# A causal attention layer's prologue reordered: value copies on ScalarE, second-batch products in other banks and among the first maxima, stacks loaded by parts, centring done one stage earlier

## The chip, the cores and the metric

The kernel runs on one core of one Trainium2 chip. The metric is the device time of one execution in microseconds (us); lower is better. TensorE multiplies, VectorE and ScalarE work elementwise and reduce, GpSimd fills constants and does some elementwise work, SyncE (SP) issues the DMAs.

## The reference, cut to what matters

The program is a decoder of two layers over x of shape (2, 1024, 256). Layer 0 has linear attention, a cross attention and a recurrence; layer 1 has causal attention with 16 heads of 16 dimensions, attention to a short context, and a routed mixture of experts. What the change touches is the end of the recurrence and the start of the causal attention:

```python
h = layernorm(x)                              # over the 256 features
q, k, v = h @ Wq + bq, h @ Wk + bk, h @ Wv + bv   # 16 heads of 16
scores = q @ k.T / sqrt(16)                   # per batch and head, 1024 x 1024
probs = softmax(where(causal, scores, -inf))
x = x + (probs @ v) @ Wout + bout
```

The line is a summary; the kernel computes it with features on the partitions and tokens along the free dimension (`c.xT`, 128 x 2 x 2048).

## The kernel before, in words

Each layer is a stage with a block of its own, in which each engine has one written-out order of instructions, tied to the others by semaphores; a stage starts on all engines when the one before has ended. The tokens fall into four chunks of 512 (`ch` 0 to 3; 0 and 1 are batch 0).

**The end of the recurrence** (`cross_attention_and_recurrence`). TensorE's order ends with `mean(bn, 0)`, `mean(bn, 1)`, `variance(bn, 0)`, `outputs(1, 1)` and `variance(bn, 1)` (L1163 to L1168): the statistics of the next norm, for batch 0 alone. VectorE adds the outputs to x (`add_output`, L1434), sums both feature halves (`add_halves`, L1398), centres chunks 0 and 1 (`centre`, L1402) and multiplies them by the inverse root (`normalise_tokens`, L1409). ScalarE makes the roots (L1225, L1228).

**The prologue of the causal layer** (`causal_attention_layer`). TensorE makes the means of the late chunks 2 and 3 (L1793), the queries of batch 0 (L1813, banks 0 to 3), the variances of the late chunks (L1804), the keys (L1813, banks 4 to 7) and the values (L1820, banks 0 to 3 again, once the queries are read); then the same for batch 1: queries into banks 0 to 3, each once VectorE has copied the values of batch 0 out of the bank (`v_copied`), keys into banks 4 to 7, and values into banks 0 to 3. An f32 product of 128 x 512 is two passes on TensorE, so four products of two halves are 16 passes. VectorE centres the late chunks (L2020), ScalarE squares them (L1958) and, between queries and keys, takes their roots (`late_roots`, L1963 and L1966), and VectorE scales them (L2026).

ScalarE reads queries and keys out of PSUM with their bias (L1977). For batch 0 it then makes the splitting copies: each of q and k is cut into three bf16 parts, the first two by ScalarE (L1986), each followed by VectorE's subtraction (L2032, then L2034, which writes the third). GpSimd does the same for batch 1 later (L1775 to L1781), once batch 0's parts are stored. VectorE copies the values of both batches into `v_aug` (L2041), after its last subtraction.

SP stores the six parts of batch 0 to DRAM (L1724), waits for all six, and loads them back as stacks (`loads`, L1717 and L1719): a quad is four heads, its stack of q and of k holds six blocks of 16 partitions, block r being part `Q_PART[r]` or `K_PART[r]`:

```python
Q_PART = (0, 0, 0, 1, 1, 2)
K_PART = (0, 1, 2, 0, 1, 0)
```

So a quad is twelve DMAs of 128 KB. Quad 0 and quad 1 are issued one after the other, then SP waits for the first shift rows (`keep_shift`, L1730), then issues quad 2, whose stack lies where the normalised tokens were, so that it waits for the last values. There are three stacks for the eight quads of both batches.

**The main loop.** Before TensorE can make a score (L1860), the row maxima of that half must be known. A maximum product or "piece" (`piece`, L1838 with a mask product L1841) is reduced by VectorE (L2051); after the eleven pieces of the first half VectorE splits the negated maxima (`split_shift`, L2065, L2067), TensorE turns them (L1848), VectorE copies them out (L2074) and SP's two small DMAs put them as two rows under the query stack (L1730). Rows of ones under the key stacks are GpSimd's memsets (L1766 for the first two stacks, L1770 for the third, which lies in the weights' room and waits for the last values). `count_pieces` plans how many pieces stand before each score; twelve stand before the first. TensorE's order ahead of the loop, before:

```python
pe.wait_ge(*s["masks"](2))
pe.wait_ge(*s["k_ones"](2))
pe.wait_ge(*pr["k_raw"](4))
pe.wait_ge(*pr["v_copied"](4))
more_pieces(0, upto[0])
```

`k_ones` reaches 2 with GpSimd's second memset. The pieces go through a ring of four banks (4 to 7), the scores through banks 0 to 2. ScalarE takes the exponentials (L1994) and TensorE multiplies them with the values (L1875).

Of the kernel before, what the change touches and what calls it, by code (L numbers as in the profile page):

```python
# [28 lines left out]
P = 128  # L29
# [668 lines left out]
def cross_attention_and_recurrence(nc, c):  # L698
# [42 lines left out]
    with ExitStack() as ctx:  # L741
# [81 lines left out]
        with nc.Block() as block:  # L823
# [46 lines left out]
            def _(pe):  # L870
# [297 lines left out]
                variance(bn, 1)  # L1168

# [140 lines left out]
            def _(dve):  # L1310
# [251 lines left out]
                add_output(1, 1)  # L1562
                for ch in (0, 1):
                    normalise_tokens(bn, ch)
# [3 lines left out]
def causal_attention_layer(nc, c):  # L1568
# [81 lines left out]
    with ExitStack() as ctx:  # L1650
        bn, yn = c.bn, c.yn
        pr = c.signals(nc, "bp", dict(q_proj=4, k_proj=4, v_proj=4, q_raw=4, k_raw=4, v_copied=4))
        s = c.signals(nc, "b", dict(part=0, rest=0, last_part=0, stored=0, later_part=0, later_stored=0, ones=0, masks=0, k_ones=0,
                                       loaded0=0, loaded1=0, loaded2=0, shifted0=0, shifted1=0, made=0, read=0,
                                       max_step=0, parts=0, scored=0, expd=0, av=0, out_copied=0, inv=0))
        set_round(0, s)
        loaded = [s["loaded0"], s["loaded1"], s["loaded2"]]
        shifted = [s["shifted0"], s["shifted1"]]
        sb = lambda name, shape, dt=F32: ctx.enter_context(nc.sbuf_tensor(name, shape, dt))
# [42 lines left out]
        with nc.Block() as block:  # L1702

            @block.sync
            def _(sync):
                def loads(n):
                    b, quad = divmod(n, QUADS)
                    a = n % 3
                    if n == 2:
                        pr["v_proj"].round = 1  # L1710
                        sync.wait_ge(*pr["v_proj"](4))
                    if n >= 3:
                        sync.wait_ge(*s["scored"](QUAD * first_group(2 * (n - 2))))
                    by_head = lambda ap: ap.rearrange("(h d) n -> d h n", d=DH)
                    rows = slice(quad * QUAD * DH, (quad + 1) * QUAD * DH)
                    for r in range(len(Q_PART)):
                        sync.dma_start(qs[a][r * DH:(r + 1) * DH], by_head(q_dram[b, Q_PART[r], rows, :]))\  # L1717
                            .then_inc(loaded[a].sem, 16)
                        sync.dma_start(ks[a][r * DH:(r + 1) * DH], by_head(k_dram[b, K_PART[r], rows, :]))\  # L1719
                            .then_inc(loaded[a].sem, 16)  # L1720
# [34 lines left out]
            def _(pool):  # L1755
# [11 lines left out]
                pr["v_proj"].round = pr["q_raw"].round = pr["k_raw"].round = 1  # L1767
                pool.wait_ge(*pr["v_proj"](4))
                pool.wait_ge(*s["k_ones"](1))
                pool.memset(ks[2][ROWS:ROWS + SHIFT], 1.0).then_inc(s["k_ones"].sem)  # L1770
                pool.wait_ge(*s["stored"](6 * 16))
                pool.wait_ge(*s["k_ones"](2))
                for n, (raw, parts, ready) in enumerate(((raw_of[1][0], q_parts, pr["q_raw"]), (raw_of[1][1], k_parts, pr["k_raw"]))):
                    pool.wait_ge(*ready(4))
# [7 lines left out]
                pool.wait_ge(*s["later_part"](8))  # L1782
                for ch in range(3):
# [6 lines left out]
            def _(pe):  # L1790
                for ch in LATE:
                    pe.wait_ge(*bn["sum"](ch + 1))
                    pe.matmul(norm_bank(ch), c.mean_w[:], factor(ch), start=True, stop=True).then_inc(bn["mean"].sem)  # L1793
                for b in range(B):
                    set_round(b, pr)
                    xn = lambda k, first, n: xn_all[:, k, b * S + first:b * S + first + n]
                    for name, base, done in (("b_wq", 0, pr["q_proj"]), ("b_wk", 4, pr["k_proj"])):
                        for n in range(4):
                            m, j = divmod(n, NCH)
                            if b == 0 and base and n == 0:  # L1800
                                for ch in LATE:
                                    pe.wait_ge(*bn["sq"](ch + 1))
                                    for k in range(FT):
                                        mm = pe.matmul(norm_bank(ch), c.mean_w[:], squares[ch][:, k, :], start=(k == 0), stop=(k == 1))  # L1804
# [1694 lines left out]
```

## Time and profile before

| what | value |
|---|---|
| three runs | 1653.85, 1656.48, 1660.8 us |
| median | 1656.48 us |
| the profiled execution's own time | 1651.91 us |
| its span | 1650.2 us |
| mean granted TensorE clock in it | 0.968 |
| busy in the span | TensorE 93%, VectorE 58%, ScalarE 44%, GpSimd 23% |

The profile is of one execution, in us from the start of its span. "PE" is TensorE's multiplying, "PEld" its loading of weights, DVE is VectorE, ACT ScalarE, POOL GpSimd, SP or SPq SyncE and its queue of DMAs. A granted clock of 1.00 is the full 2.4 GHz, 0.50 is 1.2 GHz. L1838 is line 1838 of the kernel. The causal layer starts at 708.3 us.

### The profile page before, as it was taken

What the parts mean: (1) busy time and instruction counts of PE and PEld (TensorE: products, weight loads), DVE (VectorE), ACT (ScalarE), POOL (GpSimd) and SP (SyncE); (2) the same over time, 40 slices, a digit from 0 to 9 for tenths busy, and PEclk for the clock granted to TensorE, in tenths of its full rate; (3) what the DMA queues carried; (4) which work ended last, traced back from release to release, by engine and by line L of the source; (5) the groups of instructions that cost most, each with busy time, mean ns of one, the idle gap of its engine ahead of it and who ended that gap; (6) DMA issues with size and microseconds to landing.
All of it is one profiled execution on the core that took longest, in us unless ns stands there. A gap on an engine that the chain in (4) does not pass through costs nothing. (4 is left out here: it accounts for less than half of the span.)

```text
span 1650.2 us, 19104 instructions
## 1 busy us (share of the span) xinstructions
PE 1533.0 (93%) x6998; PEld 838.9 (51%) x7002; DVE 962.3 (58%) x1491; ACT 718.6 (44%) x1256; POOL 372.2 (23%) x300
## 2 busy tenths in 40 slices
PE   6989999998999999977999999889879999999998
PEld 3744444432222234434454544332358888888886
DVE  4642124767675652343978776368579575564753
ACT  4345232453334333251466566533555444545441
POOL 0000000122221210034200000110216655655561
PEclk9989999999999999987999999989999999999998
DMA  6000000000000000017255330000302332312201
GB/s 274 1 1 0 0 0 4 1 0 1 1 0 1 1 0 0 0 68 98 28 128 67 40 40 2 1 4 1 103 26 77 98 100 73 103 65 88 84 9 51
DMA packets 38707, 67.54 MB, mean 41 GB/s; under 512 B 3864, under 2 KB 19288, under 8 KB 38232
## 3 DMA queue, kind: packets, MB, share of 16 engines
q1 hardware_dynamic: 38616, 66.33, 15.6%
q8 instruction: 56, 0.92, 0.2%
q14 instruction: 35, 0.29, 0.1%
HBM read 57.80 MB, written 8.39 MB: 40 GB/s over the span
## 5 line engine op out<-in xcount | busy, mean ns | idle before, releaser
L1994 ACT ACTIVATE arena<-psum 128x512 f32<-128x512 f32 (+3 forms) x384 | 164.8, 498 | 131.0 <-PE psum L1863 97.5
L2051 DVE TENSOR_REDUCE b_mx<-psum 128x1 f32<-128x512 f32 (+3 forms) x304 | 181.3, 653 | 44.3 <-PE psum L1841 34.8
L2794 POOL TENSOR_TENSOR m_w_rest<-m_w,m_w_high 128x512 fp32r<-128x512 f32 (+1 forms) x88 | 112.6, 1281 | 159.4 <-ACT m_w_high L2991 159.4
L3230 DVE TENSOR_TENSOR m_hidden<-m_gelu,psum 128x512 f32<-128x512 f32 (+1 forms) x88 | 60.4, 686 | 143.6 <-ACT m_gelu L3079 122.5
L2885 PE MATMUL psum<-m_x_high,m_w_high 128*128 128x512 f32 (+1 forms) x352 | 137.2, 390 | 2.9 <-issue 2.9
L2885 PE MATMUL psum<-m_x_rest,m_w_high 128*128 128x512 f32 (+1 forms) x352 | 137.0, 389 | 0.0
L2885 PE MATMUL psum<-m_x_high,m_w_rest 128*128 128x512 f32 (+1 forms) x352 | 137.0, 389 | 0.0
L2800 POOL TENSOR_TENSOR m_h_rest<-m_hidden,m_h_high 128x512 fp32r<-128x512 f32 (+1 forms) x88 | 122.0, 1387 | 58.0 <-ACT m_h_high L3005 58.0
L1203 ACT ACTIVATE x_probs<-psum 128x1024 f32<-128x1024 f32 x64 | 65.5, 1023 | 135.9 <-PE psum L955 135.9
L1346 DVE TENSOR_REDUCE x_mx<-psum 128x2 f32<-128x1024 f32 x64 | 77.0, 1219 | 51.2 <-PE psum L929 51.1
L3079 ACT ACTIVATE m_gelu<-psum 128x512 f32<-128x512 f32 (+1 forms) x88 | 52.4, 596 | 119.0 <-PE psum L2885 119.0
L1838 PE MATMUL psum<-b_k_stack,b_q_stack 96*128 96x512 bf16 (+3 forms) x288 | 89.4, 341 | 6.5 <-POOL weights_sb L1770 3.7
L1860 PE MATMUL psum<-b_q_stack,b_k_stack 98*128 98x512 bf16 (+3 forms) x288 | 90.0, 331 | 5.4 <-DMA b_q_stack<-b_stage 3.1
L3005 ACT ACTIVATE m_h_high<-m_hidden 128x512 fp32r<-128x512 f32 (+1 forms) x88 | 55.7, 633 | 81.5 <-DVE m_hidden L3230 81.5
L968 PE MATMUL psum<-x_probs,arena 128*64 128x512 f32 x256 | 71.0, 633 | 8.5 <-ACT x_out L1213 8.5
L955 PE MATMUL psum<-arena 64*128 64x512 f32 x256 | 74.8, 662 | 0.0
L2885 PEld LDWEIGHTS psum<-m_x_high,m_w_high 128*128 128x128 f32 (+1 forms) x352 | 65.0, 185 | 17.9 <-issue 3.2
L1875 PE MATMUL psum<-arena,weights_sb 128*32 128x512 f32 (+3 forms) x768 | 73.3, 500 | 0.0
L2885 PEld LDWEIGHTS psum<-m_x_high,m_w_rest 128*128 128x128 f32 (+1 forms) x352 | 65.0, 185 | 15.0
L2885 PEld LDWEIGHTS psum<-m_x_rest,m_w_high 128*128 128x128 f32 (+1 forms) x352 | 65.0, 185 | 14.9
L2898 PE MATMUL psum<-m_h_high,m_o_high 128*128 128x512 f32 (+1 forms) x176 | 72.3, 411 | 0.2 <-POOL m_h_rest L2800 0.2
L2898 PE MATMUL psum<-m_h_high,m_o_rest 128*128 128x512 f32 (+1 forms) x176 | 68.8, 391 | 0.0
(546 smaller groups left out, 3008.1 us busy)
## 6 DMA issues: line engine op xcount, KB each, us to landing
m_w<-w SPq DMA_DIRECT2D x32, 512.0 KB, 4.6
m_wo<-wo SPq DMA_DIRECT2D x16, 512.0 KB, 3.9
weights_sb<-weights SPq DMA_DIRECT2D x2, 2820.0 KB, 12.2
m_w<-w SPq DMA_DIRECT2D x16, 344.0 KB, 5.0
b_q_stack<-b_q_dram SPq DMA_DIRECT2D x36, 128.0 KB, 6.8
b_k_stack<-b_k_dram SPq DMA_DIRECT2D x36, 128.0 KB, 7.3
weights_sb<-weights SPq DMA_DIRECT2D x1, 3328.0 KB, 13.6
b_q_dram<-b_q_parts SPq DMA_DIRECT2D x6, 512.0 KB, 3.7
```

Of the source, the lines that this page charges most:

```text
L955: mm = pe.matmul(to[0:keys, h, :], k, qt[b][rows, m, half * CH:(half + 1) * CH], start=False, stop=True)
L968: mm = pe.matmul(out_tile[h * DH:(h + 1) * DH, :], v, probs[slot % RING][0:keys, h, :], start=(kt == 0), stop=(kt == TT))
L1346: dve.tensor_reduce(mx[:, n % 2, i // 2, i % 2, :], two_heads(tile(("piece", n, i))), AX, ALU.max).then_inc(s["read"].sem)
L1838: mm = pe.matmul(bank[:, x * keys:(x + 1) * keys], qs[n % 3][0:ROWS, h, qi * P:(qi + 1) * P], ks[n % 3][0:ROWS, h, first:first + keys], st ...
L1860: mm = pe.matmul(score(slot)[:, 0:n], ks[a][0:ROWS + SHIFT, h, ki * P:(ki + 1) * P], qs[a][0:ROWS + SHIFT, h, q0:q0 + n], start=True, stop ...
L1875: mm = pe.matmul(out_tile[h * PAD:(h + 1) * PAD, CH - n:CH], v_aug[:, b * TT + ki, quad * QUAD + h, :], probs[(QUAD * (2 * pair + i) + h) ...
L1994: act.activation(probs[slot % RING][:, 0:n], score(slot)[:, 0:n], ACT.Exp, scale=SCALE).then_inc(s["expd"].sem)
L2051: dve.tensor_reduce(mx[:, part, qi, heads[0]:heads[0] + nh], tile(("piece", p))[:, 0:nh * keys].rearrange("p (h n) -> p h n", n=keys), AX, ...
L2794: pool.tensor_tensor(w_rest[:, n % W_RING, :, :, 0:H_N(n % HT)], raw_of(n), w_high[:, n % W_RING, :, :, 0:H_N(n % HT)].bitcast(F32), ALU.s ...
L2800: pool.tensor_tensor(h_rest[rows, n % H_RING, :], hidden[rows, n % 2, :], h_high[rows, n % H_RING, :].bitcast(F32), ALU.subtract).then_inc ...
L2885: mm = pe.matmul(c.bank(base + n % 2)[0:H_N(h), :], of[:, k, :], x_of[ex % 2][:, k, :], start=(k == 0 and i == 0), stop=(k == FT - 1 and i ...
L2898: mm = pe.matmul(total(m), of[rows, n % O_RING, m * P:(m + 1) * P], h_of[rows, n % H_RING, :], start=(h == 0 and i == 0), stop=(h == HT - ...
```

## The change

Four things are changed together.

- The means and the centring of the late chunks (`mean(bn, 2)`, `mean(bn, 3)` and their `centre`) move to the end of the recurrence; in the causal layer TensorE starts with the queries, ScalarE with the squares.
- The values are copied out of PSUM by ScalarE: three copies of batch 0 between and behind its splitting copies, the others after the keys of batch 1.
- Batch 1's queries go into banks 4 to 7, once batch 0's keys are read, its keys into banks 0 to 3, once batch 0's values are copied. Its first two value groups follow; the other two stand among the first maxima, after four and after eight pieces. The pieces no longer wait for the second memset: that wait (`k_ones` 2) stands before the first score of the fifth half, and the memset itself behind GpSimd's splitting of batch 1.
- Quad 0 is loaded by parts, each as soon as the two stores of that part have landed, with a semaphore for each part, and between the stores. The other quads are loaded part by part too, in one go. The change is in the order: the number of DMAs is the same.

```diff
@@ cross_attention_and_recurrence: tensor
                 variance(bn, 1)
+                mean(bn, 2)
+                mean(bn, 3)
@@ vector
                 add_output(1, 1)
+                for ch in (2, 3):
+                    dve.wait_ge(*bn["mean"](ch + 1))
+                    centre(ch, mean_bank(ch), bn["cent"])
                 for ch in (0, 1):
                     normalise_tokens(bn, ch)
@@ causal_attention_layer: sync
-                def loads(n):
+                def load_part(n, i):
...
                     for r in range(len(Q_PART)):
...
+                        if Q_PART[r] == i:
+                            sync.dma_start(qs[a][r * DH:(r + 1) * DH], by_head(q_dram[b, i, rows, :])).then_inc(loaded[a].sem, 16)
+                        if K_PART[r] == i:
+                            sync.dma_start(ks[a][r * DH:(r + 1) * DH], by_head(k_dram[b, i, rows, :])).then_inc(loaded[a].sem, 16)
+
+                def loads(n):
+                    if n == 2:
+                        sync.wait_ge(*pr["v_proj"](8))
+                    if n >= 3:
+                        sync.wait_ge(*s["scored"](QUAD * first_group(2 * (n - 2))))
+                    for i in range(3):
+                        load_part(n, i)
...
-                for i in range(3):
-                    for n in range(2):
-                        sync.wait_ge(*(s["part"](2 * i + n + 1) if i < 2 else s["last_part"](n + 1)))
-                        store(0, n, i, s["stored"])
-                sync.wait_ge(*s["stored"](6 * 16))
-                loads(0)
+                for n in range(2):
+                    sync.wait_ge(*s["part"](n + 1))
+                    store(0, n, 0, stored[0])
+                sync.wait_ge(*s["part"](3))
+                store(0, 0, 1, stored[1])
+                sync.wait_ge(*stored[0](2 * 16))
+                load_part(0, 0)
+                sync.wait_ge(*s["part"](4))
+                store(0, 1, 1, stored[1])
+                for n in range(2):
+                    sync.wait_ge(*s["last_part"](n + 1))
+                    store(0, n, 2, stored[2])
+                for i in (1, 2):
+                    sync.wait_ge(*stored[i](2 * 16))
+                    load_part(0, i)
                 loads(1)
@@ gpsimd
-                pool.wait_ge(*pr["v_proj"](4))
+                for done in stored:
+                    pool.wait_ge(*done(2 * 16))
                 pool.wait_ge(*s["k_ones"](1))
-                pool.memset(ks[2][ROWS:ROWS + SHIFT], 1.0).then_inc(s["k_ones"].sem)
-                pool.wait_ge(*s["stored"](6 * 16))
-                pool.wait_ge(*s["k_ones"](2))
...
                 pool.wait_ge(*s["later_part"](8))
+                pool.wait_ge(*pr["v_proj"](8))
+                pool.memset(ks[2][ROWS:ROWS + SHIFT], 1.0).then_inc(s["k_ones"].sem)
+                pool.wait_ge(*s["k_ones"](2))
@@ tensor
+                for n in range(4):
+                    project_in(0, "b_wq", n, c.bank(n), pr["q_proj"])
                 for ch in LATE:
...
+                for n in range(4):
+                    if n in LATE:
+                        pe.wait_ge(*bn["log"](n + 1))
+                    project_in(0, "b_wk", n, c.bank(4 + n), pr["k_proj"])
+                for t2 in range(4):
+                    pe.wait_ge(*pr["q_raw"](t2 + 1))
+                    value(0, t2)
+                pe.wait_ge(*bn["out"](B * NCH))
+                for n in range(4):
+                    pe.wait_ge(*pr["k_raw"](n + 1))
+                    project_in(1, "b_wq", n, c.bank(4 + n), pr["q_proj"])
+                for n in range(4):
+                    pe.wait_ge(*pr["v_copied"](n + 1))
+                    project_in(1, "b_wk", n, c.bank(n), pr["k_proj"])
+                later_value(0)
+                later_value(1)
...
                         pe.wait_ge(*shifted[hs % 2](SHIFT * 16 * (hs // 2 + 1)))
+                        if hs == 4:
+                            pe.wait_ge(*s["k_ones"](2))
...
                 pe.wait_ge(*s["masks"](2))
-                pe.wait_ge(*s["k_ones"](2))
-                pe.wait_ge(*pr["k_raw"](4))
-                pe.wait_ge(*pr["v_copied"](4))
-                more_pieces(0, upto[0])
+                pe.wait_ge(*pr["q_raw"](8))
+                more_pieces(0, 4)
+                later_value(2)
+                more_pieces(4, 8)
+                later_value(3)
+                more_pieces(8, upto[0])
+                pe.wait_ge(*s["k_ones"](1))
+                pe.wait_ge(*pr["v_copied"](8))
@@ scalar
+                def copy_value(b, t2):
+                    act.wait_ge(*pr["v_proj"](4 * b + t2 + 1))
+                    act.activation(v_aug[:, b * TT + 2 * t2:b * TT + 2 * t2 + 2, :, 0:DH],
+                                   c.bank(t2).rearrange("p (t h d) -> p t h d", t=2, h=H), ACT.Copy).then_inc(pr["v_copied"].sem)
...
+                        act.activation(parts[:, i, :, :], raw_of[0][n], ACT.Copy).then_inc(s["part"].sem)
+                        if (i, n) == (0, 1):
+                            copy_value(0, 0)
+                        elif i == 1:
+                            copy_value(0, n + 1)
+                copy_value(0, 3)
+                for n in range(4):
+                    keep(1, raw_of[1][0], n, c.bank(4 + n), "b_bq", pr["q_proj"], pr["q_raw"])
+                for n in range(4):
+                    keep(1, raw_of[1][1], n, c.bank(n), "b_bk", pr["k_proj"], pr["k_raw"])
+                for t2 in range(4):
+                    copy_value(1, t2)
@@ vector
-                for ch in LATE:
-                    dve.wait_ge(*bn["mean"](ch + 1))
-                    for k in range(FT):
-                        ins = dve.tensor_tensor(chunk(xn_all, ch)[:, k, :], chunk(c.xT, ch)[:, k, :], norm_bank(ch), ALU.subtract)
-                    ins.then_inc(bn["cent"].sem)
...
-                dve.wait_ge(*s["ones"](1))
-                for b in range(B):
-                    set_round(b, pr)
-                    for t2 in range(4):
-                        dve.wait_ge(*pr["v_proj"](t2 + 1))
-                        dve.tensor_copy(v_aug[:, b * TT + 2 * t2:b * TT + 2 * t2 + 2, :, 0:DH],
-                                        c.bank(t2).rearrange("p (t h d) -> p t h d", t=2, h=H)).then_inc(pr["v_copied"].sem)
```

`later_value(t2)` waits until ScalarE has read key bank t2 of batch 1 and then makes value group t2 in it; `project_in`, `value` and `keep` hold the product and the reading that stood in the loops before, unchanged.

## Rows read from the trace of the kernel before

**Rows 1.** The page, part 1: busy us, share of the span, instructions.
```profile
PE 1533.0 (93%) x6998; PEld 838.9 (51%) x7002; DVE 962.3 (58%) x1491; ACT 718.6 (44%) x1256; POOL 372.2 (23%) x300
```

**Rows 2.** Windows: start:end, us, busy by engine, PEclk, DMA share, GB/s.
```profile
741.90:769.00 27.10, 23.43 (x65) 13.04 (x66) 4.39 (x7) 5.50 (x8) 3.53 (x2) 0.88 0.99 133
...
830.00:900.00 70.00, 69.08 (x611) 34.92 (x610) 55.12 (x109) 46.37 (x114) 0.00 (x0) 1.00 0.53 102
```

**Rows 3.** Waits from 702 to 775 us: total, times, longest.
```profile
POOL weights_sb L1770 <- PE psum L1820: 42.2, 1, 42.2
...
PE psum L1813 <- DVE weights_sb L2041: 5.3, 1, 5.3
```

**Rows 4.** Timeline, 765 to 781 us: start, us, instruction, [idle before <-releaser].
```profile
765.34 3.51 POOL L1770 MEMSET weights_sb<- 2x4096 bf16 x1 [42.19 <-PE psum L1820]
...
768.95 0.27 PE L1838 MATMUL psum<-b_k_stack,b_q_stack 96*128 96x128 bf16 x1 [3.67 <-POOL weights_sb L1770]
...
770.00 6.22 DVE L2051 TENSOR_REDUCE b_mx<-psum 128x4 f32<-128x512 f32 x11 [3.99 <-PE psum L1841]
...
777.35 0.38 PE L1848 MATMUL psum<-ident,b_shift 128*8 128x128 bf16 x4 [2.37 <-DVE b_shift L2067]
...
778.21 1.44 SPq L1730 DMA_DIRECT2D b_q_stack<-b_stage  x2
...
780.79 0.61 PE L1860 MATMUL psum<-b_q_stack,b_k_stack 98*128 98x512 bf16 x1 [3.06 <-DMA b_q_stack<-b_stage]
```

**Rows 5.** Both stacks' tiles (issues, landings, query stack first) and a store's landing.
```profile
L1717 SPq DMA_DIRECT2D b_q_stack<-b_q_dram x12: 334/426/427, 744.8 to 755.1; - x12
...
DMA to landing us min/median/max: 3.0/9.9/16.5
...
L1719 SPq DMA_DIRECT2D b_k_stack<-b_k_dram x12: 426/426/432, 745.2 to 755.5; - x12
...
DMA to landing us min/median/max: 3.7/10.4/16.8
...
b_q_dram<-b_q_parts SPq DMA_DIRECT2D x3, 512.0 KB, 2.7
```

**Rows 6.** Timeline, 705 to 712 us: the seam of the two stages.
```profile
705.48 2.50 DVE L1409 TENSOR_TENSOR weights_sb<-weights_sb,ln 128x512 f32<-128x512 f32 x4 [3.10 <-ACT ln L1228]
...
708.31 3.75 PE L1793 MATMUL psum<-ln,mean_w 128*128 128x512 f32 x4 [6.38 <-PEq L823]
...
710.39 1.28 DVE L2020 TENSOR_TENSOR weights_sb<-xT,psum 128x512 f32<-128x512 f32 x2 [2.41 <-PE psum L1793]
```

**Rows 7.** Windows of the prologue, finer; columns as in rows 2.
```profile
708.30:712.90 4.60, 4.59 (x6) 2.00 (x7) 2.09 (x4) 1.06 (x1) 4.60 (x1) 0.51 0.01 4
...
740.00:742.00 2.00, 0.13 (x1) 0.16 (x1) 2.00 (x3) 0.00 (x0) 0.00 (x0) 0.53 1.05 397
...
747.00:765.00 18.00, 18.00 (x59) 10.83 (x57) 2.08 (x3) 4.81 (x7) 0.00 (x0) 1.00 1.09 123
769.00:774.00 5.00, 5.00 (x29) 3.49 (x30) 4.00 (x8) 0.00 (x0) 4.92 (x2) 0.50 0.34 39
774.50:777.80 3.30, 0.85 (x7) 0.33 (x5) 3.23 (x7) 0.00 (x0) 3.16 (x3) 0.98 0.00 0
780.80:784.40 3.60, 3.60 (x17) 1.95 (x18) 2.08 (x4) 1.19 (x2) 3.52 (x3) 0.50 1.05 152
```

**Rows 8.** Timeline from 730 us, and ScalarE's PSUM reading from the grouped lines.
```profile
730.30 1.90 ACT L1986 ACTIVATE b_q_parts<-arena 128x2048 bf16<-128x2048 f32 x1
...
732.23 2.29 DVE L2032 TENSOR_TENSOR arena<-arena,b_q_parts 128x2048 f32<-128x2048 f32 x1 [4.23 <-ACT b_q_parts L1986]
...
741.04 2.48 DVE L2041 COPY weights_sb<-psum 128x512 f32<-128x512 f32 x4
...
758.21 7.07 PE L1820 MATMUL psum<-weights_sb 128*128 128x256 f32 x32
...
L1977 ACT ACTIVATE arena<-psum,vectors_sb 128x512 f32<-128x512 f32 x12 | 8.1, 683 | 9.0 <-PE psum L1813 9.0
```

More of the change, by code:

```diff
@@ new lines, in _, with project_in, value @@
+                xn = lambda b, k, first, n: xn_all[:, k, b * S + first:b * S + first + n]
+                def project_in(b, name, n, bank, done):
+                    m, j = divmod(n, NCH)
+                    for k in range(FT):
+                        mm = pe.matmul(bank, c.w(name, k, m * P, P), xn(b, k, j * CH, CH), start=(k == 0), stop=(k == 1))
+                    mm.then_inc(done.sem)
+                def value(b, t2):
+                    for t in (0, 1):
+                        for k in range(FT):
+                            mm = pe.matmul(c.bank(t2)[:, t * D:(t + 1) * D], xn(b, k, (2 * t2 + t) * P, P),
+                                           c.w("b_wv", k, 0, D), start=(k == 0), stop=(k == 1))
+                    mm.then_inc(pr["v_proj"].sem)
@@ new lines, in later_value @@
+                def later_value(t2):
+                    pe.wait_ge(*pr["k_raw"](4 + t2 + 1))
+                    value(1, t2)
+                for n in range(4):
+                    project_in(0, "b_wq", n, c.bank(n), pr["q_proj"])
+                for ch in LATE:
+                    pe.wait_ge(*bn["sq"](ch + 1))
+                    for k in range(FT):
+                        mm = pe.matmul(norm_bank(ch), c.mean_w[:], squares[ch][:, k, :], start=(k == 0), stop=(k == 1))
+                    mm.then_inc(bn["var"].sem)
@@ new lines, in keep @@
+                def keep(b, t, n, bank, bias, ready, done):
+                    m, j = divmod(n, NCH)
+                    act.wait_ge(*ready(4 * b + n + 1))
+                    act.activation(t[:, m, j * CH:(j + 1) * CH], bank, ACT.Identity, bias=c.v(bias, m)).then_inc(done.sem)
+                def copy_value(b, t2):
+                    act.wait_ge(*pr["v_proj"](4 * b + t2 + 1))
+                    act.activation(v_aug[:, b * TT + 2 * t2:b * TT + 2 * t2 + 2, :, 0:DH],
+                                   c.bank(t2).rearrange("p (t h d) -> p t h d", t=2, h=H), ACT.Copy).then_inc(pr["v_copied"].sem)
@@ new lines, in _ @@
+                for n in range(4):
+                    keep(0, raw_of[0][0], n, c.bank(n), "b_bq", pr["q_proj"], pr["q_raw"])
+                late_roots()
+                for n in range(4):
+                    keep(0, raw_of[0][1], n, c.bank(4 + n), "b_bk", pr["k_proj"], pr["k_raw"])
+                act.wait_ge(*s["ones"](1))
+                for i in range(2):
+                    for n, parts in enumerate((q_parts, k_parts)):
+                        if i == 0:
+                            act.wait_ge(*pr["k_raw" if n else "q_raw"](4))
+                        else:
+                            act.wait_ge(*s["rest"](n + 1))
+                        act.activation(parts[:, i, :, :], raw_of[0][n], ACT.Copy).then_inc(s["part"].sem)
[3 more added lines that the diff above has]
+                            copy_value(0, n + 1)
```

68 lines of the change are left out of this document (6 added, 62 removed).

## The prediction, made before the changed kernel was run

> **What bounds the kernel now.** The page first: TensorE is busy 93% of the span [rows 1], so only stretches in which it waits, or runs at the lower of its two clock levels, can give time back. The windows put one such stretch at the head of the causal layer: from 741.9 to 769.0 us the DMA engines are at 0.99 and the granted clock is 0.88, while later, from 830 to 900 us, TensorE is busy 69.08 of 70 us at clock 1.00 [rows 2]. Everything after about 790 us is in order of TensorE's own work; I take it to move as a block. The waits of the prologue name what ends last [rows 3]: TensorE stands 5.3 us for VectorE's copy of the first values (L2041), then, after all products of the second batch, for a GpSimd memset (L1770) that itself had waited 42.2 us for the last values. In the timeline that memset runs from 765.34 to 768.85, the first maximum product follows after 3.67 us of standing, and the first score (L1860) starts at 780.79 [rows 4]. That instant is my yardstick: whatever it moves, the end moves.
>
> What is already there by then? The 24 stack loads of quads 0 and 1 are issued from 744.8 to 755.5 us; the first lands 3.0 us after its issue, the last 16.8 us after it [rows 5], so they land one after another from 747.8 to 772.3: (772.3 - 747.8)/23 = 1.065 us each. Quad 0's twelve are in at 759.5. The 9.4 us up to 768.95 are lost because the first maxima stand behind the second batch's products. The change moves them out of that place; then the loads of quad 0 end last.
>
> **The parts, worked out.**
>
> *Centring in the recurrence.* VectorE waits 3.10 us there before L1409 and starts at 705.48 [rows 6]. Two centrings of 2 x 0.64 us (L2020 took 1.28 us for such a pair) cost 2.6 us. The mean products follow TensorE's last variance (ends 701.9) and the sum of 702.4: first mean ready at 702.8, centrings from 702.8 to 705.4. I take 0; without the gap it would be 2.6 us, and the end kept for the range is 0.2 us. In the causal layer four cold passes (3.75 us with their tail) vanish in front of the queries [rows 6]. The clock came back at 712.9 [rows 7], so what is saved is four passes at the full clock, 4 x 0.43 = 1.7 us. The squares now start with the stage, nine us ahead of their use, and are off the path. ScalarE's first splitting copy, at 730.30 [rows 8], comes at 728.6.
>
> *Values copied by ScalarE.* VectorE's copy is 0.62 us of a group of four (2.48 us), ScalarE's reading of such a bank is 0.683 us [rows 8]. Three copies come into the splitting chain. Copies at 1.90 us, subtractions at 2.29: q part 0 ends 730.5, k part 0 732.3, value copy 733.0 (q's rest is ready at 732.8, so this costs 0.2), q part 1 734.9, copy 735.6, k part 1 737.5; the last subtraction ends 739.8, where before VectorE came to the value copies at 741.04. Cost on this chain 0.4 us of the 1.7 gained. VectorE is left with nothing to copy and the 5.3 us stall goes.
>
> *Second batch's products in other banks.* TensorE ends the first batch's values at 734.7 and finds the key banks long read. 32 passes x 0.43 = 13.7 us, no fall of the clock (the stall had cost one; clock 0.53 from 740 to 742, [rows 7]), then two value groups of 1.72 us (7.07 us for four, [rows 8]): TensorE is done at 752.0. Before it was done at 765.3. The other two groups now stand between the maxima.
>
> *Stacks by parts.* The price is all in the DMA queue. Stores: 512 KB at 397 GB/s [rows 7] is 1.3 us of transfer, 2.7 us from issue to landing [rows 5]. SP's order: k part 0 issued 732.3, landed 735.0; q part 1 issued 734.9, through at 737.6; six loads, issued from 735.0 (0.47 us apart, 2.8 us of SP's time), through at 737.6 + 6.4 = 744.0. The three stores left stand behind them: 3 x 1.3, so 747.9; six more loads 6.4, so 754.3. Between stores and dependent loads a bubble is possible, as SP waits for a landing; two stores (2.6 us) cover the first load's 3.0 us, so 0.5 us: **quad 0 complete at 754.8**. TensorE waits 2.8 us for it. Quad 1's twelve loads follow to 767.6.
>
> No row shows a load beside a store. Below, a load could cost nothing beside a store (different directions): 3.9 us less; above, its price could double. I take 1.065, from 24 loads in a row.
>
> The loads run at 123 GB/s with the engines saturated, the stores at 397 [rows 7]. The Trainium skill (SBUF — State Buffer, Door 1: The DMA port swizzle) says DMA speed goes by how many of 16 ports the partitions reach; each load writes 16 partitions, four ports of 436 GB/s in all sixteen, an estimate of 109 GB/s. By it twelve loads would take 1.6 us more and the result would be 1647.1; the measured rate is above it and is used.
>
> *Maxima to first score.* Before: 11.84 us from first product to first score, of which 7.3 until the eleventh maximum and 4.6 for shift, turn, copy and a 2.6 us transfer [rows 4]. TensorE stays at the full clock over an idle 2.37 us and is at 0.50 after one of 3.06 us and of 3.67 us [rows 4, 7]; 2.8 us lies between, and I take the slow one. Then its first 5.2 us are at 1.2 GHz (level 0.50): four maxima 2.5 us, values group 2 3.1, four maxima 0.9, group 3 1.8, and the last three arrive so that the eleventh maximum ends after 10.5 instead of 7.3 us. First score 15.0 us after 754.8: **769.8**, 11.0 us before 780.8. At the full clock it would be ready after 12.6 us, but the shift's 4 KB stand behind quad 1 in the queue until 767.6, so about 767.9, 12.9 us.
>
> *Moved waits.* GpSimd's splitting of batch 1 starts at 748 instead of 769 and its second memset comes at about 776; it is wanted at the fifth half, after 815, as is quad 2. Should that cover go, the memset is 3.5 us. SP's quad 2 loads follow the shift, 5.6 us of issue, wanted as late. VectorE's maxima then lie beside no GpSimd work; they took the same time with and without it, so 0.
>
> Sum: the profiled execution took 1651.91 us (span 1650.2 and 1.7 around it); less 11.0 it is 1640.9. It lay 4.6 us under the median of 1656.48, so on the median: **1645.5 us**. Of the 11.0, 1.3 come from the centring and chain, the rest from the prologue's order.
>
> **Rivals.**
>
> *Quad 0 lands late* (17%). If the queue shares its engines among waiting transfers, quad 0 ends towards quad 1's end: between 754.8 and 767.6, the first score between 770 and 782.6, gain 11 to -1.8, in the middle 4.6: 1651.9. For: quad 1 is issued while quad 0's last parts move. Against: the first of 24 loads landed after 3.0 us though eleven more were issued behind it [rows 5], which is an order. The Trainium skill (DMA: Bandwidth & Descriptors, Queues, rings and completion order) says descriptors are taken in ring order but a later one may finish its write first; the landings here rise in order.
>
> *The gain is not passed on* (8%), the change then doing less than it says: the first score is early but the loop is held by the maxima of VectorE or by a late clock. It gains half, 5.5: 1651.0. Against: the loop starts from the same state whenever it starts, and TensorE is at 69.08 of 70 later [rows 2].
>
> *Loads dearer among stores* (7%, slower). All 24 loads stand before the first score's shift rows. With a load at p us, quad 1 ends at 742.0 + 24p; from p = 1.62 that is past 780.8, and from 1.97 it costs over 0.5%. At twice the price, 2.13, it is 793.1: 12.3 us slower, 1668.8. For: no row shows loads beside stores or just-written rows. Against: most of quad 0 and all of quad 1 run with no store about, as before.
>
> **How the numbers follow.** A measurement can tell 0.5%, 8.3 us. Forecast 68%: all between 8.3 and 13.5 us of gain. Late quad 0 and lost gain, 25%, lie mostly within 8.3 us: same. Slower 7%. Low end: full clock, no bubble, 13.4 us gained (1643.1), and 3 us for the scatter of medians (the three runs span 7 us): 1640. High end: the first two rivals to a gain of 3.5 us, 1653. The forecast's own range is 1640 to 1649.
>
> **What would show it.** Value copies of some 0.68 us on ScalarE between its splitting copies, and 0.2 us of waiting at each at most; TensorE without a gap from 708 to 752 and full clock from 713; first maximum product at 755, not bound by GpSimd but by a DMA; DMA engines saturated from 738 to 768; first score at 768 to 770; from there the same loop. A first product past 760 means the load order or price is wrong; a first score past 775 with maxima in time, the shift's queueing; an early score with an unchanged end, the second rival.

## The result, and the profile after

The changed kernel took 1642.37 us in the median of six runs (1639.97 to 1647.24); the kernel before, in six, 1654.86 us (1650.81 to 1660.8). The ratio is 0.9929 with a 95% interval of 0.9907 to 0.9951: 11.7 us less, between 8.1 and 15.4. In a second session it was 0.9912 (0.9891 to 0.9933).

The profiled execution is the slowest of its six, 1647.24 us with a span of 1645.5 us, and it came to the causal layer 4.5 us later than that of before, 712.8 instead of 708.3 us, for reasons in the layers ahead that the change does not touch (from 400 to 500 us, for one, its granted clock was 0.93 where it had been 1.00). So all instants below are counted from the causal layer's start, which is GpSimd's first memset (L1756 before, L1775 after). Four of them make the yardstick of this study:

| us from the layer's start | before | changed | changed, second trace |
|---|---|---|---|
| ScalarE's first splitting copy | 22.0 | 20.9 | 19.7 |
| first maximum product | 60.6 | 46.3 | 45.0 |
| VectorE's tensor_scalar for the shift begins | 68.0 | 56.2 | 53.3 |
| first score product | 72.52 | 62.75 | 61.31 |
| from there to the last `b_wo` product | 290.9 | 290.9 | 290.9 |

The last row, called the loop below, is what lets the first score stand for the whole: the main loop moved as a block. The first score came 9.8 us earlier in the one trace and 11.2 us in the other, both within the interval of the times.

The timeline of TensorE, VectorE, GpSimd and SP in the changed kernel, first from the layer's start to the first maxima (start us, us, engine and line, in brackets the idle time before and what ended it), where [rows 4, 6, 8] stood before:

```profile
707.36 2.48 DVE L1404 TENSOR_TENSOR weights_sb<-xT,psum 128x512 f32<-128x512 f32 x4 [0.44 <-PE psum L1006]
710.02 2.50 DVE L1411 TENSOR_TENSOR weights_sb<-weights_sb,ln 128x512 f32<-128x512 f32 x4 [0.18 <-ACT ln L1230]
...
712.85 9.93 PE L1815 MATMUL psum<-weights_sb 128*128 128x512 f32 x16 [4.67 <-PEq L823]
...
739.83 13.90 PE L1815 MATMUL psum<-weights_sb 128*128 128x512 f32 x32
753.56 3.62 PE L1821 MATMUL psum<-weights_sb 128*128 128x256 f32 x16
759.09 0.22 PE L1867 MATMUL psum<-b_k_stack,b_q_stack 96*128 96x128 bf16 x1 [1.91 <-DMA b_q_stack<-b_q_dram]
```

The centrings (L1404) fit in front of the scaling, which waits 0.18 us where it had waited 3.10; from the recurrence's last variance product to the layer's start it is 8.2 us in both kernels. TensorE has no gap from 712.85 to 757.2; the 5.3 us stall of [rows 3] is gone. The first maximum is released by a DMA, not by the memset of [rows 4], after 1.91 us. Then, from the same timeline:

```profile
767.08 1.89 DVE L2089 TENSOR_REDUCE b_mx<-psum 128x1 f32<-128x512 f32 x3 [0.69 <-PE psum L1870]
767.38 4.05 POOL L1793 TENSOR_TENSOR arena<-arena,b_k_parts 128x2048 f32<-128x2048 f32 x1
...
769.00 2.47 DVE L2103 TENSOR_SCALAR b_shift<-b_mx 128x16 bf16<-128x16 f32 x1
771.50 0.18 DVE L2105 SCALAR_TENSOR_TENSOR b_shift<-b_mx,b_shift 128x16 bf16<-128x16 f32 x1
...
771.82 0.59 PE L1877 MATMUL psum<-ident,b_shift 128*8 128x128 bf16 x4 [4.01 <-DVE b_shift L2105]
...
772.89 1.44 SPq L1740 DMA_DIRECT2D b_q_stack<-b_stage  x2
...
775.56 0.59 PE L1891 MATMUL psum<-b_q_stack,b_k_stack 98*128 98x512 bf16 x1 [3.15 <-DMA b_q_stack<-b_stage]
```

Here something new stands on the path. A tensor_scalar over 128x16 elements takes 2.47 us, and ends at 771.47, 0.04 us after GpSimd's subtraction of the keys (767.38 + 4.05 = 771.43). The group of all sixteen such instructions shows that it is no price of the operation (duration in ns, minimum, median, maximum):

```profile
L2103 DVE TENSOR_SCALAR b_shift<-b_mx x16: 174/175/2466, 769.0 to 1017.5; 128x16 bf16<-128x16 f32 x16
```

The windows of the changed kernel (us, then busy time by engine, granted clock, DMA share, GB/s) show the queue and the clock:

```profile
744.00:746.00 2.00, 2.00 (x6) 0.92 (x5) 0.54 (x1) 0.98 (x2) 0.00 (x0) 1.00 1.07 131
...
748.00:750.00 2.00, 2.00 (x6) 0.93 (x5) 0.00 (x0) 0.69 (x1) 0.00 (x0) 1.00 1.01 369
750.00:752.00 2.00, 2.00 (x6) 0.92 (x5) 0.00 (x0) 0.69 (x1) 0.00 (x0) 1.00 1.05 406
...
760.00:764.00 4.00, 4.00 (x18) 3.14 (x17) 2.25 (x4) 0.00 (x0) 3.92 (x2) 0.63 1.10 152
764.00:768.00 4.00, 3.81 (x24) 2.52 (x21) 3.01 (x6) 1.19 (x2) 3.92 (x3) 1.00 1.06 124
768.00:770.00 2.00, 0.00 (x0) 0.00 (x0) 1.97 (x3) 0.00 (x0) 2.00 (x1) 0.94 0.19 25
```

The queue goes in order: six loads at 131 GB/s, then the three stores behind them at 369 to 406, then loads again to 768.4, from 742 on at a share above 1.0. TensorE's clock falls to 0.50 some 0.4 us after it took up work at 759.09, for about 3.4 us (the mean of 0.63 from 760 to 764 is that fall).

### The profile page after: what moved, and what is told of

Read it like the earlier page. It is cut to its first block and busy times, and to the rows that moved or that the text cites. A ratio compares the mean times of both kernels' runs of the same rounds, so it can differ in the third digit from the quotient of the medians.

```text
span 1645.5 us, 19104 instructions
## 1 busy us (share of the span) xinstructions
PE 1533.0 (93%) x7002; PEld 839.1 (51%) x7002; DVE 958.7 (58%) x1483; ACT 722.2 (44%) x1264; POOL 372.3 (23%) x300
## 5 line engine op out<-in xcount | busy, mean ns | idle before, releaser
L2089 DVE TENSOR_REDUCE b_mx<-psum 128x1 f32<-128x512 f32 (+3 forms) x304 | 181.5, 653 | 58.5 <-PE psum L1870 48.9
L2832 POOL TENSOR_TENSOR m_w_rest<-m_w,m_w_high 128x512 fp32r<-128x512 f32 (+1 forms) x88 | 112.6, 1282 | 159.6 <-ACT m_w_high L3029 159.6
L1348 DVE TENSOR_REDUCE x_mx<-psum 128x2 f32<-128x1024 f32 x64 | 77.0, 1220 | 57.2 <-PE psum L929 57.1
L968 PE MATMUL psum<-x_probs,arena 128*64 128x512 f32 x256 | 70.5, 629 | 8.5 <-ACT x_out L1215 8.5
```

The costliest lines, as they stand in the source:

```text
L968: mm = pe.matmul(out_tile[h * DH:(h + 1) * DH, :], v, probs[slot % RING][0:keys, h, :], start=(kt == 0), stop=(kt == TT))
L1348: dve.tensor_reduce(mx[:, n % 2, i // 2, i % 2, :], two_heads(tile(("piece", n, i))), AX, ALU.max).then_inc(s["read"].sem)
L2089: dve.tensor_reduce(mx[:, part, qi, heads[0]:heads[0] + nh], tile(("piece", p))[:, 0:nh * keys].rearrange("p (h n) -> p h n", n=keys), AX, ...
L2832: pool.tensor_tensor(w_rest[:, n % W_RING, :, :, 0:H_N(n % HT)], raw_of(n), w_high[:, n % W_RING, :, :, 0:H_N(n % HT)].bitcast(F32), ALU.s ...
```

## The experiments

The theory after the result: the path to the first score is the centring and splitting chain, then quad 0's loads in an order of the queue, then the maxima; and it ends in a lock between VectorE and GpSimd, whose work the change moved side by side: a small VectorE instruction does not finish before the GpSimd instruction that was running when it began. The rivals were other causes for each part. Each kernel's distance from the layer's start to the first score is given, the yardstick of the expectations; for single runs the time itself says little, since runs of one kernel lie up to 12 us apart.

### The centring alone

The kernel before, with the first hunks of the diff (`mean(bn, 2)` and `(bn, 3)`, two centrings) and the same instructions taken out of the causal layer.

> The kernel before with the centring of the late chunks moved into the recurrence, and nothing else. Yardstick for all runs here: us from the causal layer's start (GpSimd's first memset) to the first score product; before 72.5, changed kernel 62.7. Theory (the prediction's): the recurrence does not grow, four cold passes go, ScalarE's first splitting copy comes 1.7 us earlier after the stage's start, 20.3 instead of 22.0, but it is absorbed here, since the first maxima wait for TensorE's values and the memset, whose own chain shortens by the same 1.7: yardstick 70.8. Rival (read from the changed kernel's trace, where the splitting began only 1.1 us earlier): the clock returns later after the stage's start, yardstick 71.4.

Measured: splitting at 19.6, first maximum at 58.7, first score at 70.5 us: 2.0 us of gain, 0.3 us from the theory's 70.8 and 0.9 from the rival's 71.4. The splitting itself began 2.5 us earlier, not 1.7. TensorE still stands 5.29 us for L2038, as before.

### Value copies back on VectorE

```diff
...
-                        if (i, n) == (0, 1):
-                            copy_value(0, 0)
-                        elif i == 1:
-                            copy_value(0, n + 1)
-                copy_value(0, 3)
...
+                dve.wait_ge(*s["ones"](1))
+                for t2 in range(4):
+                    copy_value(0, t2)
+                copy_value(1, 0)
+                copy_value(1, 1)
...
+                more_pieces(0, 8)
+                copy_value(1, 2)
+                more_pieces(8, upto[0])
+                copy_value(1, 3)
```

> The changed kernel with the value copies back on VectorE: batch 0's four and batch 1's first two before the maxima, the other two after the eighth and the twelfth maximum. Banks, load order and all else as in the changed kernel. Theory 1 (the move to ScalarE only shortens a stall that the other banks remove anyway): batch 1's keys find the banks read in time, no gap on TensorE, quad 0 complete within 0.5 us of the changed kernel, yardstick 62.7 plus or minus 1. Theory 2 (the copy's engine matters in itself): TensorE stands again at batch 1's keys, some 3 us or more, and the yardstick is 65 or more.

Measured: no gap on TensorE at the keys, first maximum at 44.7, 0.3 us before the changed kernel's second trace. Theory 1 in this. But the first score came at 57.1, earlier than either theory had it. The reason is in its timeline:

```profile
767.20 0.17 DVE L2101 TENSOR_SCALAR b_shift<-b_mx 128x16 bf16<-128x16 f32 x1
...
765.45 1.89 POOL L1791 CAST b_k_parts<-arena 128x2048 bf16<-128x2048 f32 x1
767.42 4.08 POOL L1793 TENSOR_TENSOR arena<-arena,b_k_parts 128x2048 f32<-128x2048 f32 x1
```

The tensor_scalar starts in the last 0.14 us of GpSimd's cast and ends 0.05 us before the subtraction begins. A few tenths later it would have waited for all of it, as in the changed kernel's second trace.

### Quad 0 loaded after all stores

```diff
...
-                load_part(0, 0)
-                sync.wait_ge(*s["part"](4))
-                store(0, 1, 1, stored[1])
...
+                for i in range(3):
+                    for n in range(2):
+                        sync.wait_ge(*(s["part"](2 * i + n + 1) if i < 2 else s["last_part"](n + 1)))
+                        store(0, n, i, stored[i])
+                for done in stored:
+                    sync.wait_ge(*done(2 * 16))
+                loads(0)
```

> The changed kernel with quad 0's twelve loads issued only after all six stores have landed, as before. Theory 1 (the prediction's: quad 0 ends last, and the loads by parts fill the queue while it would stand idle): last store lands 35 us after the stage's start, first load 3.0 us later, eleven more at 1.0: quad 0 complete at 49 to 50 instead of 46.3, TensorE idle before the first maximum 5 us instead of 1.9, yardstick 65.5 to 66.5. Theory 2 (the queue has the same bytes to move in either order): no later than 1 us, yardstick 62.7 to 63.7.

Measured: TensorE waits 5.65 us for the load, the first maximum comes at 48.9 and the first score at 66.6. That is theory 1. The parts are worth 2.6 to 3.8 us at the first maximum. The first score says less here: the clock was at 0.50 when the maxima began, and the tensor_scalar was held too, for 2.64 us, to the end of GpSimd's memset.

### All of GpSimd's splitting held until after the first shift

```diff
                 pool.wait_ge(*s["k_ones"](1))
+                pool.wait_ge(*s["parts"](1))
```

> The changed kernel, with GpSimd's splitting of batch 1 held until VectorE has written the first half's split shift. In the changed kernel VectorE's small tensor_scalar (L2103, 128x16) took 2.47 us and ended 0.04 us after GpSimd's subtraction; later ones took 0.17. Theory 1 (VectorE's instruction is locked out while GpSimd's holds their shared port): it takes 0.2 us, the yardstick falls by 2.3 us to 60.4, the whole kernel by the same 2.3 us against the changed one; GpSimd's splits, 24 us later at most, are still in time. Theory 2 (it was slow for another reason, such as a code fetch or its first use): it stays at 2 us or more and the yardstick at 62.7. Theory 3 (the shift's 4 KB then stand behind quad 1 in the queue): the instruction is short, but the rows land no earlier, yardstick 62 to 62.7.

Measured: the first tensor_scalar took 0.18 us and the first score came at 58.0. Theory 1's mechanism, with more than its 2.3 us, since the clock did not fall here either; theory 2, first use, and theory 3, the queue, both fall. Yet the whole was no better: ratio 0.9952 (0.9932 to 0.9972) against the kernel before, and the loop took 298.7 instead of 290.9. The timeline says where most of the 7.8 us went:

```profile
781.10 4.07 DVE L2101 TENSOR_TENSOR b_mx<-b_mx 128x16 f32<-128x16 f32 x1
785.20 3.54 DVE L2104 TENSOR_SCALAR b_shift<-b_mx 128x16 bf16<-128x16 f32 x1
788.77 0.17 DVE L2106 SCALAR_TENSOR_TENSOR b_shift<-b_mx,b_shift 128x16 bf16<-128x16 f32 x1
...
781.08 4.06 POOL L1798 TENSOR_TENSOR b_k_parts<-arena,b_k_parts 128x2048 bf16<-128x2048 f32 x1
785.19 3.51 POOL L1801 MEMSET weights_sb<- 2x4096 bf16 x1
```

The late splitting now met the second half's shift. Its two small instructions, 0.18 and 0.17 us elsewhere, took 4.07 and 3.54 us, each to within 0.04 us of the end of a GpSimd instruction that had begun 0.01 to 0.02 us before it. TensorE stood 8.09 us for VectorE there, and worked at 0.50 afterwards; it never waited for a load of batch 1's stacks. "Still in time" was right for the stores and wrong for the lock.

### The changed kernel once more

> The changed kernel itself once more, for a second trace and for times beside the runs below. In its first trace the clock fell to 0.50 after the first four maximum products and VectorE's tensor_scalar was held 2.3 us until GpSimd's key subtraction ended. Two kernels of the first batch of runs with the same order up to there kept the clock. If the fall is chance, this trace has the tensor_scalar about 54 us after the stage's start, within GpSimd's key cast or at the start of its subtraction, and the yardstick lies between 57.5 and 62.7. If the fall belongs to the order of the work, it is 62.7 again.

Measured: first maximum at 45.0, tensor_scalar at 53.3 us, and GpSimd's key subtraction had begun 0.17 us before it:

```profile
764.51 3.92 DVE L2103 TENSOR_SCALAR b_shift<-b_mx 128x16 bf16<-128x16 f32 x1
...
764.34 4.06 POOL L1793 TENSOR_TENSOR arena<-arena,b_k_parts 128x2048 f32<-128x2048 f32 x1
```

It was held for 3.92 us, to the subtraction's end. First score at 61.3: the clock had stayed at its full level through the maxima this time, after an idle 1.88 us. So the fall in the first trace does not come from the order of the work alone, and it did not add its full cost, because the lock's end does not move with the tensor_scalar's start.

### Only the keys' splitting held

```diff
...
+                    if n == 1:
+                        pool.wait_ge(*s["parts"](1))
                     pool.wait_ge(*ready(8))
```

> The changed kernel with GpSimd's splitting of batch 1's keys alone held until the first half's split shift is written; the queries' splitting runs as early as in the changed kernel. Theory (one shared port): the first tensor_scalar takes 0.2 us since GpSimd is idle then, GpSimd ends its last subtraction and memset about 69 us after the stage's start, before the second half's shift at 75, so that takes 0.2 us too. Yardstick 57.5 to 58.5, the loop after it 290.8 as in the changed kernel; the whole 2 to 4 us under the changed one. Rival (what cost 7.8 us in the run with all splitting held was the lateness of batch 1's parts for the stores, not the port): the loop is longer than 291.5 here as well, by a part of those 7.8.

Measured: first score at 57.5, loop 290.9.

```profile
766.52 0.17 DVE L2105 TENSOR_SCALAR b_shift<-b_mx 128x16 bf16<-128x16 f32 x1
...
787.32 0.18 DVE L2102 TENSOR_TENSOR b_mx<-b_mx 128x16 f32<-128x16 f32 x1
787.53 0.17 DVE L2105 TENSOR_SCALAR b_shift<-b_mx 128x16 bf16<-128x16 f32 x1
...
766.97 1.89 POOL L1793 CAST b_k_parts<-arena 128x2048 bf16<-128x2048 f32 x1 [2.49 <-DVE b_shift L2107]
...
779.15 3.51 POOL L1802 MEMSET weights_sb<- 2x4096 bf16 x1
```

GpSimd waits 2.49 us, is done at 782.7, and both shifts find GpSimd idle or waiting. That is 3.8 us less to the first score than in the changed kernel's second trace, and the rival, late parts, falls with the loop's 290.9. The times, on the same chip and beside the same runs of before: 1642.03 us in the median of four, ratio 0.9902 (0.9878 to 0.9927), against 1643.92 us and 0.9912 (0.9891 to 0.9933) for the changed kernel. By the medians it is 1.9 us, at the low end of the 2 to 4 expected. The intervals overlap; the 3.8 us are shown by the traces, and the times don't contradict them and don't prove them.

### Both findings together

Copies on VectorE as above and the keys' splitting held.

> Value copies on VectorE and the keys' splitting held: what both findings give together. Expected: splitting 0.4 us earlier, quad 0 complete 45 us after the start, yardstick 57.0 to 58.0, loop 290.8, the whole level with or up to 1 us under the run that only holds the keys, and 13 us or more under the kernel before. If the second batch's copies between the maxima hurt, the yardstick is 58.5 or more.

Measured: splitting at 20.9, first maximum 46.2, tensor_scalar 54.5 (0.17 us), first score 58.5, loop 289.3; 1641.53 us in the median of four, ratio 0.9899 (0.9878 to 0.9921). The clock came back late at the layer's start here, as in the changed kernel's first trace: TensorE's first sixteen passes took 9.93 us, against 8.73 in its second. So the 58.5, at which the expectation had the copies do harm, doesn't show that: from first maximum to first score it is 12.3 us, as in the kernel with the keys held. By its centre it is the best of the versions, but no better than the last one can be told.

### Batch 1 in the banks as before

The two `project_in` loops of batch 1 with queries in banks 0 to 3 behind `v_copied`, keys in 4 to 7 behind `k_raw`; the rest as changed.

> The changed kernel with batch 1's products in the old banks (queries 0 to 3 behind the value copies, keys 4 to 7), copies on ScalarE and all else as changed. Theory: either part alone, copies on ScalarE or other banks, removes TensorE's 5.3 us stall; here the copies are there 0.1 to 0.5 us after TensorE wants them: TensorE is done with batch 1's second value group at most 1 us later, quad 0's loads still end last, yardstick as in the changed kernel (57.5 to 62.7 by the clock and the port). Rival: the banks carry the gain; then a gap of 3 us or more stands before batch 1's queries and the first maximum comes at 48 or later.

Measured: the 32 passes take 13.90 us, as changed, with no gap; first maximum at 44.7, tensor_scalar at 53.0 for 4.07 us, first score at 61.1. With the kernel that had the value copies back on VectorE, either part alone removes the stall; the rival falls.

### All values ahead of the maxima

> The changed kernel with all four value groups of batch 1 ahead of the first maxima instead of two of them between. Theory (the groups fill a wait for quad 0's loads, so it is nearly free where they stand): TensorE is done 46.4 us after the stage's start, when the loads are in too (45 to 46.3); first maximum at 46.5, VectorE's eleven in 7.2 us, tensor_scalar at 53.8 against 53.3 to 56.2 in the changed kernel; it falls into GpSimd's key subtraction and waits to about 57.3; yardstick 61.3. The clock can't fall, since TensorE has no idle time ahead of the maxima. Rival (interleaving hides 3.4 us of TensorE's work): first maximum at 48 or later, yardstick 64.

Measured: first maximum 46.5, tensor_scalar 53.4 for 3.89 us, first score 61.3, as the theory had it to 0.5 us in each. Two groups between the maxima or ahead of them make no difference.

### The maxima behind the memset again

As the last one, with `pe.wait_ge(*s["k_ones"](2))` ahead of the maxima and the memset ahead of GpSimd's splitting.

> As the run with the values first, but with the first maxima behind GpSimd's second memset and that ahead of its splitting, as in the kernel before; copies, banks, load order and centring as changed. Theory (the port): values done at 46.4, memset to 49.9, first maximum at 50.0, tensor_scalar at 57.3; GpSimd's splits begin 10 us later than in the changed kernel, so that it meets the end of a cast, 0.5 us, as in the kernel before; yardstick 61.9 to 62.5, the same as the changed kernel's within 1 us: what the free order of the maxima gains, the port takes back. Rival (no port): the tensor_scalar is as long as in the changed kernel, 2.5 us or more, and the yardstick 64 or more.

Measured: memset from 46.8 to 50.3, first maximum at 50.6, tensor_scalar at 57.4, first score at 62.5. Its timeline:

```profile
765.59 0.99 DVE L2100 TENSOR_SCALAR b_shift<-b_mx 128x16 bf16<-128x16 f32 x1
...
764.66 1.89 POOL L1798 CAST b_q_parts<-weights_sb 128x2048 bf16<-128x2048 f32 x1
766.63 4.08 POOL L1800 TENSOR_TENSOR b_q_parts<-weights_sb,b_q_parts 128x2048 bf16<-128x2048 f32 x1
```

The maxima start 5.5 us later than in the changed kernel's second trace, and the first score is only 1.2 us later. Here the tensor_scalar met a cast and waited 0.8 us. In the kernel before it was the same with 735 ns, until the cast's end: the lock was in the profile that I predicted from.

## Why the prediction was right or wrong

**The size was right, in part by luck: a lock left out and a fall of the clock taken for certain nearly cancelled.** Forecast 1645.5 us, 11.0 below the median, with a range of 1640 to 1649; measured 1642.37, 11.7 below, with 8.1 to 15.4. First score: forecast 11.0 us earlier, measured 9.8 and 11.2. The order of events up to the first maximum was as forecast; from there to the first score it was not.

**Centring.** "I take 0" held: 0.18 us of waiting left, and the stage seam is where it was. The four passes: forecast 1.7 us at the splitting copy, measured 1.1, 2.3 and, alone, 2.5. The term moves with the clock's return at the layer's start: sixteen passes took 8.60 to 9.93 us over these kernels, with the same 4.67 us of idle before them.

**Copies on ScalarE.** They take 0.58 us each in the chain, not 0.683. The last subtraction ends 31.7 us after the start, against a forecast of 31.5. What I had not seen is that they buy nothing beside the other banks: each of the two alone removes the stall.

**Loads by parts.** Quad 0 complete at 754.8 by the forecast, which is 46.5 from the start; measured 46.3 and 45.0. Quad 1's twelve loads land from 759.8 to 770.0 us in the first trace, 0.93 us apart, somewhat less than 1.065, and the six ahead of the stores move at 131 GB/s. The order of the queue is as assumed, so the late-quad rival and the dearer-loads rival both fall. The Trainium skill's port rule, by which I had an estimate of 109 GB/s (SBUF — State Buffer, Door 1: The DMA port swizzle), lies below the 124 to 152 GB/s here; where they differ, the measurement decides.

**Maxima to first score: the step that failed.** I wrote that "VectorE's maxima then lie beside no GpSimd work" and put the term at 0. They lie beside all of it: the splitting runs from 40.5 to 64.8 us after the start. I had its begin, 748, and the end of the memset behind it, 776, and did not lay them beside the maxima. I had also left the 0.73 us tensor_scalar within the 4.6 us as if that were its price, while fifteen of its kind take 0.17. The lock cost 2.3 us in the first trace, 3.7 in the second.

What hid the error is a second one: I took the fall of the clock for certain, which is 15.0 us from first maximum to first score instead of 12.6. It came in the first trace, where the tensor_scalar began 9.9 instead of 8.3 us after the first maximum product, and not in the second nor in the five other kernels with this order of loads, after 1.65 to 2.02 us of idle. The four kernels with neither lock nor fall took 12.3 us, near the 12.6. Forecast 15.0; measured 16.5 and 16.3, with quad 0 complete 0.2 and 1.5 us earlier than forecast. The reading behind the fall was loose as well. In the kernel before, the clock fell 0.3 us after TensorE had taken up the turn at 777.35, so behind the idle 2.37 us that I took for harmless and ahead of the 3.06 us that I blamed (windows, the clock in the third column from the end):

```profile
777.00:777.60 0.60, 0.26 (x4) 0.23 (x4) 0.58 (x2) 0.00 (x0) 0.56 (x1) 1.00 0.00 0
777.70:778.20 0.50, 0.03 (x1) 0.00 (x0) 0.48 (x2) 0.00 (x0) 0.50 (x1) 0.50 0.00 0
```

**The shift behind quad 1** decided nothing: the loads' transfers end at 768.4 and the shift was issued at 772.89. In the kernel with the keys held it was issued 1.7 us before quad 1's last landing, and TensorE waited the same 3.15 us for it.

**The cause of the long instructions** is shown by the kernels in which only GpSimd's place in time differs: 0.17 us where it is idle, and elsewhere up to the end of whichever GpSimd instruction ran, subtraction (2.47 to 4.07 us), cast (0.74 and 0.99) or memset (2.64 and 3.54), to within 0.04 us. Code fetch or first use is ruled out: the same first instruction takes 0.17 and 0.18 us in the two kernels that hold GpSimd back, and in one of them the second is held. Reductions out of PSUM were never longer, at most 0.69 us for 512 columns with or without GpSimd beside them. The Trainium skill has this (SBUF — State Buffer, Who interferes with whom): VectorE and GpSimd share a port pair that one instruction holds whole, asked for by VectorE's tensor_scalar in its fast mode and by any operation with two SBUF inputs against a GpSimd one that reads, and not by a reduction. The traces agree in each of these kinds, a 128x16 tensor_tensor held for 4.07 us by a subtraction among them; that the tensor_scalar was in its fast mode no run shows. It would have given the term, had I applied it.

**Not passed on** falls as well: 290.9 us of loop in both traces, as before.

## What to carry to other kernels

When a change moves work of GpSimd in time, lay it beside every small VectorE instruction on the path: a 0.17 us one can cost 4 us, and a moved block collides somewhere else, so move the one piece that collides. Look at minimum and maximum of a group, not its mean: an instruction that is four times its sisters and ends with another engine's is waiting. When two parts of a change remove the same stall, price them together once.

The same signs stand elsewhere in the changed kernel's trace, in the mixture of experts, and in the trace of before alike:

```profile
L3201 DVE SCALAR_TENSOR_TENSOR m_one_hot<-m_iota,m_code,arena x16: 750/752/1684, 1201.6 to 1225.8; 128x512 fp32r<-128x512 f32 x16
...
1208.90 0.47 PE L2872 MATMUL psum<-m_one_hot,m_tok_high 128*128 128x512 f32 x1 [3.15 <-DVE m_one_hot L3201]
```

From 1203.84 us on, GpSimd makes five subtractions (L2832), and L3201 and the tensor_scalar L3199 beside it, 0.75 and 0.48 us elsewhere, take 1.5 to 1.7. TensorE stands 3.15 us for them. No run here moved that GpSimd work, so that it is the lock is an inference, and what it would give back is not shown.

## What the runs showed of the hardware that was not expected

TensorE's clock is not the same from run to run after the same idle time: after 1.91 us without work it fell to 0.50 in one trace, 0.4 us after TensorE had resumed, and after 1.88, 1.89 and 2.02 us in three others it did not. Starting a layer after 4.67 us idle, the return to full clock put the end of sixteen passes anywhere from 8.60 to 9.93 us. What decides it these runs don't show.

The same clock explains why the loop took 289.3 instead of 290.9 us in two of the kernels. In every other one of the 290.9 us kind it fell to 0.50 for 3.4 us somewhere in the loop while TensorE had work, for instance 284 us after the first score in the changed kernel's first trace, 243 in the second and in the kernel before, 20 to 21 in the kernel with the values first and the one with the banks as before. Two loops had a further fall 10 us after the first score and lost nothing by it; in the second trace, where one of them stands, VectorE was busy for 14.83 of 15 us there, so TensorE was not what set the pace. In the two short loops there is no fall past the first 7 us. Half of 3.4 us is 1.7, about the 1.6 us by which they differ. The windows around the end of the loop, in the changed kernel and in the one with both findings, show it (clock 0.81 and 1.00):

```profile
1057.00:1066.00 9.00, 7.05 (x18) 3.51 (x19) 3.98 (x7) 4.20 (x6) 0.00 (x0) 0.81 0.00 0
...
1057.00:1066.00 9.00, 6.12 (x14) 2.69 (x15) 4.29 (x7) 3.02 (x4) 0.63 (x4) 1.00 0.00 0
```

So two kernels' times can differ by 1.6 us for this alone, nearly the 1.9 us that holding the keys gained in the medians.
